# The transposes of the row maxima move one slot later on PE, in an attention block on one core

## What is computed

```python
def _sln(h, w, ln_g, ln_b, Wg, bg, Wb, bb):        # LayerNorm, scaled and shifted by the condition
    ln = (h - mu) / jnp.sqrt(var + EPS) * ln_g + ln_b
    return (w @ Wg.T + bg)[:, None, :] * ln + (w @ Wb.T + bb)[:, None, :]

h = _sln(hidden, w, ...)
qkv = (h @ Wqkv.T + bqkv).reshape(B, N, 16, 16, 3)  # 16 heads of 16 channels
q, k, v = ...                                       # each [B, 16, 256, 16]
energy = jnp.einsum('bhqd,bhkd->bhqk', q, k)
att = jax.nn.softmax(energy, axis=-1) / D ** 0.5
out = jnp.einsum('bhqk,bhkd->bhqd', att, v)         # heads side by side again
h1 = out @ Wp.T + bp + hidden
return _sln(h1, w, ...) + h1
```

## Time and profile before

| | |
|---|---|
| median of 3 runs | 350.76 us (348.23 to 350.86) |
| the profiled execution | 349.5 us, of which 347.7 us are the span |
| mean granted clock of TensorE | 0.99 |
| busy, share of the span | PE 96%, PEld 83%, DVE 85%, ACT 70%, POOL 46% |

### The profile page before, as it was taken

How to read it: one execution, slowest core, us unless ns; L and a number is a source line. 1 busy time by engine, 2 the same in 40 slices (tenths; PEclk the granted TensorE clock), 3 DMA queues, 4 the chain that set the end, 5 groups by cost and what they waited for, 6 DMA issues and landing times.

```text
span 347.7 us, 8982 instructions
## 1 busy us (share of the span) xinstructions
PE 334.0 (96%) x3173; PEld 288.6 (83%) x3173; DVE 297.0 (85%) x728; ACT 242.8 (70%) x476; POOL 159.0 (46%) x187
## 2 busy tenths in 40 slices
PE   8886989999999999999999999999999999999993
PEld 4675968889898888888898888888898888888773
DVE  4874877789898989989898989989898988998684
ACT  7762686868678686868687686868687686766740
POOL 5476261525464462726454462726454453225330
PEclk9997899999999999999999999999999999999999
DMA  8487245544555465565545565656546454652011
GB/s 239 128 202 204 58 123 151 150 134 129 161 131 158 135 180 155 136 173 139 157 133 156 134 176 153 141 154 160 156 135 154 106 170 124 168 147 75 18 60 60
DMA packets 47705, 48.87 MB, mean 141 GB/s; under 512 B 6287, under 2 KB 41374, under 8 KB 47662
## 3 DMA queue, kind: packets, MB, share of 16 engines
q1 hardware_dynamic: 44782, 47.00, 49.3%
q0 software_dynamic: 1984, 0.51, 0.9%
q10 hardware_dynamic: 896, 0.80, 0.8%
HBM read 9.99 MB, written 4.23 MB: 41 GB/s over the span
## 4 chain that ended last, share of the span: by engine, by line
PE 86%; DVE 5%; ACT 2%; DMA 2%; POOL 2%; issue 2%; SPq 0%; DVEq 0%; POOLq 0%; ACTq 0%
PE m L969 24%; PE st L969 19%; PE sa L969 18%; PE pv L969 17%; PE pv L1058 4%; PE pv L1139 2%; PE m L1098 2%; DMA wqkv<-WqkvT_dram 2%; DVE mx L688 1%; DVE qk_l L723 1%; POOL qk_l L415 1%; POOL xn L378 1%; PE pv L1072 1%; PE m L1072 1%; ACT qk_h L522 0%
## 5 line engine op out<-in xcount | busy, mean ns | idle before, releaser
L688 DVE TENSOR_REDUCE mx<-sa 128x2 f32<-128x512 f32 x256 | 171.6, 683 | 30.1 <-PE sa L969 29.0
L602 ACT ACTIVATE p<-st 128x512 f32<-128x512 f32 x240 | 140.9, 598 | 38.0 <-PE st L969 33.9
L969 PE MATMUL sa<-kst,qst 126*128 126x256 f32 x512 | 106.5, 290 | 1.6 <-DVE mx L688 1.1
L969 PE MATMUL st<-qst,kst 128*128 128x256 f32 x496 | 104.0, 292 | 0.7 <-DMA qst<-m_l 0.5
L969 PEld LDWEIGHTS st<-qst,kst 128*128 128x128 f32 x496 | 75.1, 188 | 14.3 <-issue 12.8
L969 PEld LDWEIGHTS sa<-kst,qst 126*128 126x128 f32 x512 | 80.0, 193 | 3.8 <-DVE mx L688 2.1
L369 POOL DMA_DIRECT2D qst<-m_h x31 | 17.6, 566 | 117.0 <-DVE m_l L697 117.0
L969 PE MATMUL pv<-p,v_st 128*32 128x256 f32 x1008 | 61.0, 382 | 0.0
L969 PEld LDWEIGHTS pv<-p,v_st 128*32 128x32 f32 x1008 | 29.5, 109 | 21.0 <-ACT p L602 1.8
L969 PE MATMUL m<-hT_h,wqkv_h 128*128 128x256 f32 x128 | 36.8, 300 | 1.4 <-issue 0.8
L378 POOL TENSOR_SCALAR xn<-xa,mv,rstd 128x256 f32<-128x256 f32 x28 | 34.2, 1227 | 1.4
(11 more groups left out here) (149 smaller groups left out, 568.3 us busy)
## 6 DMA issues: line engine op xcount, KB each, us to landing
qst<-qk_h SPq DMA_DIRECT2D x64, 128.0 KB, 2.4
qst<-qk_l SPq DMA_DIRECT2D x64, 128.0 KB, 2.5
kst<-qk_l SPq DMA_DIRECT2D x64, 128.0 KB, 2.7
kst<-qk_h SPq DMA_DIRECT2D x62, 128.0 KB, 2.4
xa<-x_dram SPq DMA_DIRECT2D x16, 256.0 KB, 3.0
gb<-gb_rows SPq DMA_DIRECT2D x16, 256.0 KB, 3.9
out_dram<-y SPq DMA_DIRECT2D x15, 256.0 KB, 3.4
wqkv<-WqkvT_dram SPq DMA_DIRECT2D x1, 512.0 KB, 5.8
```

What stands on the lines that cost most here:

```text
L602: nc.scalar.activation(p32[:, h, :], st_ps[h % 2][:], ACT.Exp).then_inc(exp_done, 1)
L688: dve.tensor_reduce(mx[:, par(a), h // HH, (h % HH) * TT:(h % HH + 1) * TT], sa_ps[h % 2][:].rearrange("p (t n) -> p t n", t=TT), AX.X, AL ...
L969: return nc.tensor.matmul(o, l, r, start=start, stop=stop)
```

## The change

The transpose of the second half goes from slot 1 to slot 2, and within the slot to the place behind `scores_max` and in front of P.V. That of the first half goes from slot 9 to slot 10, behind `scores_max` and in front of `turn_x`, `turn_att` and P.V; only in the step b = -1 it stays in slot 9 (`M_FIRST`). ACT's `high_max` follow into slots 3 and 11. The waits in front of the transposes are the same. The orders of DVE, POOL and the DMA queue don't change.

```diff
-S_MT1, S_AT, S_MT0, S_XT = 1, 10, 9, 10
+S_MT1, S_AT, S_MT0, S_XT, M_FIRST = 2, 10, 10, 10, 9
@@ ACT, step
                 for h in range(H):
+                    if h == S_MT1 + 1 and has(b):
+                        high_max(b, 1, pv_ps[0])
                     if h == S_O1:
                         evict_out(b - 1, 1)
...
-                    if h == S_MT1 + 1 and has(b):
-                        high_max(b, 1, pv_ps[0])
-                    if h == S_MT0 + 1 and has(b + 1):
+                    if h == (M_FIRST if first(b + 1) else S_MT0) + 1 and has(b + 1):
                         high_max(b + 1, 0, pv_ps[1] if first(b + 1) else m1)
-                    if h == S_MT0 + 1 and first(b + 1):
+                    if h == M_FIRST + 1 and first(b + 1):
@@ PE, step
                     scores_max(b + 1, h)
+                    if h == (M_FIRST if first(b + 1) else S_MT0) and has(b + 1):
+                        wait(pe, h1_ready, 1 * (b - 2) + 1)
+                        wait(pe, kl_ready, B if not has(b + 2) else 1 * (b + 2) + 1 if has(b) else 1)
+                        if first(b + 1):
+                            pe.wait_ge(bias_ready, 1)
+                        transpose_max(b + 1, 0, pv_ps[1] if first(b + 1) else m1)
+                    if h == S_MT1 and has(b):
+                        wait(pe, att_ready, 2 * (b - 1) + 1)
+                        if first(b):
+                            pe.wait_ge(gbrow_ready, 1)
+                        transpose_max(b, 1, pv_ps[0])
                     if h == (X_FIRST if first(b + 1) else S_XT) and has(b + 3):
...
-                    if h == S_MT1 and has(b):
-                        wait(pe, att_ready, 2 * (b - 1) + 1)
-                        if first(b):
-                            pe.wait_ge(gbrow_ready, 1)
-                        transpose_max(b, 1, pv_ps[0])
...
-                    if h == S_MT0 and has(b + 1):
-                        wait(pe, h1_ready, 1 * (b - 2) + 1)
-                        wait(pe, kl_ready, B if not has(b + 2) else 1 * (b + 2) + 1 if has(b) else 1)
-                        if first(b + 1):
-                            pe.wait_ge(bias_ready, 1)
-                        transpose_max(b + 1, 0, pv_ps[1] if first(b + 1) else m1)
```

## The result

The changed kernel takes 350.86 us (median of 22 runs, 349.76 to 352.69), the kernel before in the same comparison 349.01 us (22 runs, 348.04 to 351.09). The ratio is 1.0049, with a 95% interval of 1.0031 to 1.0068: 0.5% slower, or 1.7 us by the ratio (the interval is 1.1 to 2.4 us; the medians differ by 1.85), where 1.6 us was forecast.

A forecast was written before the change was run, and what follows sets the result against it. DVE's work was taken to set the time from slot 3 to slot 10, PE from there to slot 3 of the next step. 1.40 + 0.2 = +1.6 us on the median 350.8 gave 352.4 us, range 349.6 to 354.6.

The forecast's parts named there:

- The pause of 0.12 us in slot 10: Slot 10 on PE: `scores_max` loads 0.12 us late because it waits for DVE's maximum of head 8.
- DVE's stretch: DVE from head 3's maximum to head 8's: no idle time from 155.10 to 162.02, so DVE's work sets the time.
- Rival B: Slot 10's pause is no wall; the first half's move costs nothing: +0.2 us, 351.0; chance 0.05.
- Moving the first half out of slot 9: Slot 9 gains nothing, slot 10 pays 0.108 us: steps of 19.61 us, 1.40 us in 13 steps.
- The second half's move is neutral: Slot 1 to slot 2 on PE: -0.12 + 0.12 = 0 us per step.
- The price of 0.12 in front of P.V: Slot 2: the transpose costs its load step of 0.135 less 0.02 of a shorter pause, 0.12 us.
- ACT hides `high_max`: Slot 11 on ACT: 0.34 us idle before the transposed attention takes in the 0.15 of `high_max`, leaving about 0.3.
- rival C: ACT becomes late in slot 11's burst, delaying exp 11 to 13: +2.0 us on top, 354.4; chance 0.08.
- The edges, +0.2: First and last steps: 0.12 in b=14, +0.07 allowed in b=1, b=0 about even; about +0.2 us.
- Rival D: Slots 2 and 10: transposes overlap nothing and cost 0.415 us each: 8.5 us on top, 360.9; chance 0.05.
- The spread of the runs sits in the start: The runs' 2.6 us spread likeliest comes from PE's clock of 0.50 for 6.8 us from 29.8 us on.
- The absolute 352.4 us: Whole kernel: forecast time set on the three runs' median of 350.8 us, 0.5% slower; chance 0.70.

The follow-up runs named there:

- a second transpose: The kernel before, with the first half's transpose done twice in slot 9: 19.50 us a step, ratio 0.9989 to the kernel before.
- the doubled transpose: The changed kernel, with the second half's transpose done twice in slot 2 in front of P.V: 19.72 us a step, ratio 1.0083 to the kernel before.
- the first remedy: DVE's statistics of the next x put ahead of head 3's maximum, in the kernel before and in the changed kernel: 19.46 and 19.60 us a step.
- second half only: The changed kernel with the first half's transpose back in slot 9, the second half's staying in slot 2: 19.51 us a step, ratio 1.0003 to before.
- statistics ahead, old order: The kernel before, with DVE's statistics of the next x ahead of head 3's maximum: 19.46 us a step, ratio 1.0000.
- the fastest kernel: The kernel before, with DVE's normalisation of the second half behind head 8's maximum: 19.39 us a step, ratio 0.9947, median 347.51 us.

## Why the prediction was right

- *The pause of 0.12 us in slot 10 is a wait for head 8's maximum.* Right. It grew when the transpose left (0.35 to 0.45 from `st` to `sa`), was filled by a second transpose, and went when DVE's stretch was shortened. Rival B, by which the first half's move costs nothing, is out with it.
- *Moving the first half out of slot 9 gains nothing, in slot 10 it costs 0.108.* Right: 19.61 us, as worked out, and 19.60 for this move alone.
- *The second half's move is neutral.* Right within 0.01 us (19.51). The price of 0.12 in front of P.V, taken from the nearest row, was met by the doubled transpose (0.11). Slot 1 got shorter by 0.10, where 0.12 was forecast.
- *ACT hides `high_max`.* Right: 0.44 us idle behind it (about 0.3 forecast), and rival C's wait did not come: the steps are 19.61 and no longer.
- *The edges, +0.2.* The sum from slot 3 of b=0 to slot 3 of b=14 is 1.64, against 1.40 + 0.2. Thirteen steps at the measured 0.113 are 1.47 of it, so about 0.17 is left for the edges. For b=14 the loads show what the prediction says: from `sa` of slot 1 to `sa` of slot 2 it is 0.93 in both kernels, and P.V comes 0.12 later behind the latter (0.43 before, 0.55 after). The other 0.05 belongs to b=0 and b=1, for which 0.07 had been allowed as an estimate.
- *Rival D, no overlap at the new places.* It would have made steps of 20.2 us (19.50 + 0.31 + 0.30, and the 0.11). The trace of after shows 0.10 from the transpose's load to the next (161.75 to 161.85), where its own load record is 0.14 and its matmul's 0.275. The Trainium skill (TensorE: Matmul & The Clock Gate, Part 3, The mechanism) says that a weight load overlaps matmuls in flight only when it goes to another row group. The trace disagrees here as it did at the old places: the next load began 0.10 us behind the transpose's, so it overlapped a matmul that uses all rows.
- *The spread of the runs sits in the start.* Right as far as the profiles show it, but only in part for its seat: the prediction names the stretch at the lower clock around 30 us, and the two groups of times go with the matmuls of the first 10 us (below).

The absolute 352.4 us came out 1.5 too high, since it was set on the median of three runs, two of which belong to the upper group of times.

One thing was drawn too simply: DVE's stretch was taken as starting at slot 3 alone. It has a second start at slot 7, only 0.05 us behind. For the change this made no difference, because both lie ahead of slot 10, but it made the first remedy fail. And 0.03 of the 0.11 us per step is not shown to be the wall's.

## What to carry to other kernels

A PE that is shown as busy for 100% of a step can still be waiting: compare the distance from load to load with the usual pace, and look for an operation elsewhere that ends just before the late load (here 0.05 to 0.06 us). Work in front of such a point is free up to the size of the pause, and work behind it costs its full time. So a move across it is not neutral, though the instructions are the same. To take such a point away, shorten the other engine's stretch behind the last place at which it can be made to wait (here slot 7), not the stretch as a whole.

## What the runs showed of the hardware

The times of one kernel fall into two groups whose medians are 2.0 us apart (the kernel before, over all comparisons: 347.8 to 350.0, and 350.3 to 351.1). The profiled execution of "second half only" fell into the upper one (351.08 us), that of the kernel before into the lower (349.5). PE's matmuls of the conditioning, at the start, first in the upper one and then in the kernel before:

```profile
6.06 1.89 PE L969 MATMUL pv<-cond,wg 128*128 128x16 f32 x8
7.79 1.87 PE L969 MATMUL m<-cond,wb 128*128 128x16 f32 x8
```
```profile
6.02 1.06 PE L969 MATMUL pv<-cond,wg 128*128 128x16 f32 x8
6.93 1.04 PE L969 MATMUL m<-cond,wb 128*128 128x16 f32 x8
```

Each set of eight matmuls takes 1.9 us instead of 1.1, and the second set ends 1.7 us later. The one other profile in the upper group ("statistics ahead, old order") has 1.89 for the first set too, and the remaining ones, all in the lower group of their kernel, have 1.06 to 1.35. So the groups go with these matmuls; what slows them is open, since the granted clock is 1.00 from 5 to 14 us in both profiles shown. Besides this there is the stretch at the granted clock of 0.50 around 29 us, of 6.8 us (before), 3.4 us (after) or none at all (the fastest kernel's profile, whose granted clock is 1.00 from 5 to 36.6 us). Both lie ahead of the pipeline's steady part. For an effect of half a per cent the length of the steps told more than 12 runs of the whole: the intervals of the ratios are 0.4 to 0.6% wide, while the steady steps of one profile lie within 0.04 us of each other.
